# Second attention and expert blocks of a four-layer kernel: which semaphore GpSimd's sums wait for, where additions to x and routing work stand in VectorE's order, and which banks the first searches use

## Reference

```python
x = x + L0_xattn(ln(x), ctx, mask)        # one head, keys and values are ctx
x = x + L0_ffn(ln(x), ...)                # 32 experts of 96, top 8 of the router's logits, softmax over the chosen
x = x + L1_xattn(ln(x), ctx, ...)         # a decayed sum over ctx, one row for each of the 4 batches
x = x + L1_ffn(ln(x), ...)                # 8 experts of 176, top 2 of sigmoid(logits) + bias, and a shared part of 352
x = x + L2_xattn(ln(x), ctx, ...)         # 16 query heads, 4 key heads of 128, 1601 + 256 keys, causal over the 256
x = x + L2_ffn(ln(x), ...)                # 4 experts of 1024, top 1
x = x + L3_xattn(ln(x), ctx, ...)
x = x + L3_ffn(ln(x), ...)
```

```python
q = rms_norm(q, q_norm_w); k = rms_norm(k, k_norm_w)
q = q * cos + rotate_half(q) * sin;  k = k * cos + rotate_half(k) * sin
out = softmax(q @ [k_ctx, k].T * scale + mask) @ [v_ctx, v];  return out @ wo
```

## Time and profile before

| | |
|---|---|
| Median of 3 runs | 2511.46 us |
| The profiled execution | 2511.3 us, span 2509.4 us, granted clock 0.983 |
| TensorE matmul busy | 2353.1 us (94%) |
| VectorE, ScalarE, GpSimd busy | 1762.4, 1733.4, 1377.6 us |
| Chain that ended last | PE 49%, DVE 24%, issue 12%, ACT 11%, POOL 2% |
| Costliest lines of the chain | DVE 1461 6%, DVE 1508 5%, PE 1619 5% |
| GpSimd's sums, line 1298 | 400 of 1559 ns |

### The profile page before, as it was taken

One profiled execution on the slowest core, in us unless ns is written; L12 is line 12 of the kernel. 1 busy time (PEld: TensorE's weight loads), 2 busy tenths in 40 slices (PEclk: granted clock), 3 DMA queues, 4 the chain that ended last, 5 costly groups with the idle time before them and its releaser, 6 DMA issues.

```text
span 2509.4 us, 53706 instructions
## 1 busy us (share of the span) xinstructions
PE 2353.1 (94%) x19062; PEld 1629.6 (65%) x19123; DVE 1762.4 (70%) x3346; ACT 1733.4 (69%) x3784; POOL 1377.6 (55%) x942
## 2 busy tenths in 40 slices
PE   7989999989999999999999999999899899999997
PEld 5677777756777777777777777777656444444434
DVE  5455767667888888888888888889621467566546
ACT  2234444447878887888878788788711488888897
POOL 1045545425666766667666676667610478778500
PEclk9989999999999999999999999999999999999999
DMA  5122322230001000010000100001310200000100
GB/s 196 56 89 82 88 83 86 70 127 18 1 17 49 18 18 2 18 49 18 18 2 18 49 18 18 2 17 41 160 47 11 72 18 19 24 16 24 53 4 18
DMA packets 42366, 108.73 MB, mean 43 GB/s; under 512 B 5060, under 2 KB 25928, under 8 KB 36936
## 3 DMA queue, kind: packets, MB, share of 16 engines
q1 hardware_dynamic: 40312, 102.28, 12.1%
q0 software_dynamic: 768, 2.10, 0.3%
q10 hardware_dynamic: 1008, 0.79, 0.1%
HBM read 99.78 MB, written 4.98 MB: 42 GB/s over the span
## 4 chain that ended last, share of the span: by engine, by line
PE 49%; DVE 24%; issue 12%; ACT 11%; POOL 2%; DVEq 1%; DMA 1%; another core or an unknown queue 0%; ACTq 0%; SPq 0%; POOLq 0%
DVE l_plo L1461 6%; DVE l_mx L1508 5%; PE psum L1619 5%; PE psum L2763 4%; PE psum L2730 3%; PE psum L2127 3%; ACT l_p L2566 3%; PE psum L2696 3%; PE psum L513 2%; PE psum L514 2%; PE psum L515 2%; PE psum L374 2%; PE psum L393 2%; ACT l_p L1341 1%; PE psum L2137 1%
## 5 line engine op out<-in xcount | busy, mean ns | idle before, releaser
L1298 POOL TENSOR_TENSOR xn<-xn,l_p 128x512 f32<-128x512 f32 (+1 forms) x400 | 623.6, 1559 | 132.4 <-ACT l_p L1341 113.5
L1461 DVE TENSOR_TENSOR l_plo<-l_p,l_phi 128x512 fp32r<-128x512 f32 (+1 forms) x464 | 457.8, 987 | 32.9 <-ACT l_phi L1340 15.7
L2566 ACT ACTIVATE l_p<-psum 128x1024 f32<-128x1024 f32 x416 | 397.7, 1036 | 54.8 <-PE psum L2730 50.1
L1340 ACT ACTIVATE l_phi<-psum 128x512 fp32r<-128x512 f32 (+1 forms) x464 | 280.7, 605 | 142.0 <-PE psum L1667 72.1
L1508 DVE TENSOR_REDUCE l_mx<-psum 128x1 f32<-128x512 f32 (+2 forms) x512 | 299.7, 615 | 10.5 <-PE psum L1714 9.9
L1352 ACT ACTIVATE psum<-l_m 128x512 f32<-128x512 f32 x461 | 286.8, 624 | 6.1
L2541 POOL TENSOR_TENSOR l_rs<-l_ms,half_power 128x32 f32<-128x32 f32 x45 | 244.4, 5432 | 68.7 <-DVE l_ms L2591 58.8
L1341 ACT ACTIVATE l_p<-psum 128x512 f32<-128x512 f32 (+1 forms) x464 | 281.3, 606 | 0.0
L2763 PE MATMUL psum<-l_p,l_vs 64*32 64x256 f32 x6656 | 251.3, 378 | 6.9 <-POOL l_vs L2537 3.0
L1648 PE MATMUL psum<-l_qThi,l_kThi 128*128 128x512 f32 (+1 forms) x464 | 233.8, 504 | 1.0 <-ACT psum L1352 1.0
L1619 PE MATMUL psum<-l_w,l_ctx 128*128 128x256 f32 (+1 forms) x832 | 218.9, 386 | 1.3 <-DVE l_vlo L1501 0.6
(11 more groups left out here) (410 smaller groups left out, 5112.5 us busy)
## 6 DMA issues: line engine op xcount, KB each, us to landing
w_stage<-in_L_w_dram SPq DMA_DIRECT2D x76, 384.0 KB, 3.1
l_w<-in_L_w_qkv_dram SPq DMA_DIRECT2D x16, 1024.0 KB, 4.8
l_ct<-in_ctx_tiles_dram SPq DMA_DIRECT2D x52, 128.0 KB, 2.1
c_T<-in_ctx_T_dram SPq DMA_DIRECT2D x4, 1601.0 KB, 7.9
l_ctx<-in_ctx_T_dram SPq DMA_DIRECT2D x4, 1601.0 KB, 6.8
c_N<-in_ctx_dram SPq DMA_DIRECT2D x4, 1536.0 KB
s_wg<-in_L_gate_dram SPq DMA_DIRECT2D x4, 1024.0 KB, 11.5
s_wu<-in_L_up_dram SPq DMA_DIRECT2D x4, 1024.0 KB, 13.6
```

Of the source, the lines that this page charges most:

```text
L1298: g_.tensor_tensor(l2_acc[k][0:r, :], first[0:r, :], l2_p[c % 3][0:r, :], ALU.add)\
L1340: act.activation(l2_phi[c % 3][0:r, :], src, ACT.Exp).then_inc(l2_e, 1)
L1461: v.tensor_tensor(l2_plo[c % 3][0:r, :], l2_p[c % 3][0:r, :], l2_phi[c % 3][0:r, :].bitcast(F32), ALU.subtract)\
L2566: act.activation(l3_p[ring(odd, c)][:, :], psum[:, (c % 2) * 2 * BANK:(c % 2 + 1) * 2 * BANK], ACT.Exp, scale=float(D3) ** -0.5).then_inc( ...
```

## The change

GpSimd's sum of a step waits for VectorE's low part of that step, not for ScalarE's exponential. The additions of the late row (k = 1) stand ahead of `prepare` in VectorE's step. `route_weights` is cut in two, `route_weights` and `route_parts`, with a table entry "parts"; for block 2 the second stands one step later, for block 3 the first moves from step 13 to 12 and the second stands at 13. In blocks 0 and 3 TensorE turns the weights before `gate_up` of the second step, not behind it. The last twelve searches ahead of turn 0 use banks 3 to 6.

```diff
-                "acted": 12, "spread": 14, "weights": 16, "table": 17},
+                "acted": 12, "spread": 14, "parts": 14, "weights": 16, "table": 17},
...
-                "logits": 18, "route": 19, "acted": 19, "spread": 20, "weights": 22, "table": 23},
+                "logits": 18, "route": 19, "acted": 19, "spread": 20, "parts": 21, "weights": 22, "table": 23},
...
-                "logits": 11, "route": 11, "acted": 12, "spread": 13, "table": 13},
+                "logits": 11, "route": 11, "acted": 12, "spread": 12, "parts": 13, "table": 13},
...
         def route_weights(v, k):
...
             if name == "L0":
                 dve_steps.then(v, v.tensor_tensor(route, a, b, ALU.subtract))
-                dve_steps.then(v, v.tensor_reduce(r_sum[:, :], route, AX.X, ALU.add))
-                dve_steps.then(v, v.reciprocal(r_sum[:, :], r_sum[:, :]))
-                dve_steps.then(v, v.tensor_tensor(route, route, wide(r_sum[:, :], E), ALU.mult))
             else:
...
                 route_topk(v, E, 2, log)
+
+        def route_parts(v, k):
...
+            if name == "L0":
+                dve_steps.then(v, v.tensor_reduce(r_sum[:, :], route, AX.X, ALU.add))
+            else:
                 dve_steps.then(v, v.tensor_tensor(route, a, b, ALU.mult))
                 dve_steps.then(v, v.tensor_reduce(r_sum[:, :], route, AX.X, ALU.add))
                 dve_steps.then(v, v.tensor_scalar(r_sum[:, :], r_sum[:, :], 1e-12, None, ALU.max))
-                dve_steps.then(v, v.reciprocal(r_sum[:, :], r_sum[:, :]))
-                dve_steps.then(v, v.tensor_tensor(route, route, wide(r_sum[:, :], E), ALU.mult))
                 dve_steps.then(v, v.memset(r_route[:, :, E:E + 1], 1.0))
+            dve_steps.then(v, v.reciprocal(r_sum[:, :], r_sum[:, :]))
+            dve_steps.then(v, v.tensor_tensor(route, route, wide(r_sum[:, :], E), ALU.mult))
...
             if at_step("spread", new, i):
                 route_weights(v, new)
+            if at_step("parts", new, i):
+                route_parts(v, new)
...
-                    if not (late and i == 1):
-                        gate_up(k, m)
+                    gate_up(k, m)
                     if late and i == 0:
                         if m - 2 >= first:
                             down(m - 2)
-                        gate_up(k, m + 1)
                         turn_weights(pe, k)
...
-        FIVE_BANKS = [FIVE[at % 5] for at in range(LAST_ON_FIVE)] + TWO_BANKS[LAST_ON_FIVE:]
+        FOUR = (3, 4, 5, 6)
+        FIVE_BANKS = [FIVE[at % 5] for at in range(LAST_ON_FIVE)] + [FOUR[(at - LAST_ON_FIVE) % 4] for at in range(LAST_ON_FIVE, len(SHARED))]
+        FIRST_LAST_IN_3 = max(SHARED[at][1] for at in range(LAST_ON_FIVE, len(SHARED)) if FIVE_BANKS[at] == 3) + 1
...
-                g_.wait_ge(l2_e, g * (3 * NS) + (3 * c + 2))
+                g_.wait_ge(l2_lo, g * NS + (c + 1))
...
+                    for half in range(2):
+                        if g is not None and c == Y_AT[1][half] and not (isinstance(g, int) and g < 1):
+                            add_out(g - 1, 1, half)
                     if n is not None:
                         prepare(c, 1 - slot, n)
...
-                                if c == Y_AT[k][half]:
-                                    add_out(g - turns_ago, k, half, LAST_Y[k][half] if last_turn(g - turns_ago) else 7)
+                                if k == 0 and c == Y_AT[0][half]:
+                                    add_out(g, 0, half, LAST_Y[0][half] if last_turn(g) else 7)
...
-            if at < 0 and banks(n)[own] == 3:
+            if at < 0 and own >= LAST_ON_FIVE and isinstance(n, int) and n == 0:
+                pe.wait_ge(h_cp, HALF_CP[1])
+            elif at < 0 and banks(n)[own] == 3:
                 pe.wait_ge(l2_o, (n - 1) * TB + 1)
...
-                if c == 0 and g > 0:
-                    pe.wait_ge(l2_far, g * NM + LAST_IN_3)
+                if c == 0:
+                    pe.wait_ge(l2_far, (g * NM + LAST_IN_3) if not isinstance(g, int) or g > 0 else FIRST_LAST_IN_3)
```

More of the change, by code:

```diff
@@ L781, in route_weights @@
             name = BLOCKS[k][0]
-            E, n_slots = MOE[name][0], MOE[name][0] + (MOE[name][2] > 0)
+            E = MOE[name][0]
             a, b, log, route = (r[:, :, 0:E] for r in (r_a, r_b, r_log, r_route))
@@ L794, in route_weights @@
                 route_topk(v, E, 2, log)
+        def route_parts(v, k):
+            name = BLOCKS[k][0]
+            E, n_slots = MOE[name][0], MOE[name][0] + (MOE[name][2] > 0)
+            a, b, route = (r[:, :, 0:E] for r in (r_a, r_b, r_route))
+            if name == "L0":
+                dve_steps.then(v, v.tensor_reduce(r_sum[:, :], route, AX.X, ALU.add))
+            else:
                 dve_steps.then(v, v.tensor_tensor(route, a, b, ALU.mult))
@@ L900, in moe_vector @@
             route_weights(v, run[0])
+            route_parts(v, run[0])
             route_table(v, run[0])
```

## The result

| | before | after |
|---|---|---|
| median of the runs (5 each), us | 2511.86 | 2523.58 |
| lowest to highest, us | 2510.0 to 2513.19 | 2519.45 to 2526.77 |
| ratio to before, 95% interval | | 1.0046 [1.0031, 1.0061] |
| profiled execution, us; its span | 2511.3; 2509.4 | 2522.44; 2520.4 |

What follows compares the result with a forecast made beforehand. TensorE was taken as nearly full, so only its waits in expert blocks, before the attention and in steps 3 to 8 could be won. 2.5 + 2.5 + 3.2 + 1.3 + 5.6 = 15.1 off 2511.3: 2496.2 us; range 2483 to 2506.

Steps and rivals of the forecast that it cites:

- The step that failed: Attention: ScalarE's exponentials wait for sums three steps on but run five us ahead of TensorE, so delays are covered.
- the sum that now stands ahead of the power in step 17: Attention, step 17: the sum between low part and power delays l2_kn, so the transposes wait 0.3 us.
- Block 0: First expert block: earlier turning of the weights lets the third gate_up start earlier; 2.5 us won, range 0 to 2.5.
- Block 1: Expert block 1, step 20: cutting routing starts VectorE's multiplications 2.0 us earlier and the next gate_up 2.5 us earlier.
- the case that I had priced at 1.9: Block 1: the half clock comes all the same, down costs 1.35 more, turning's wait covers 0.7; 1.9 us won.
- Block 2 to 3: End of block 2: routing's first half in step 12 and turning ahead of gate_up win 3.2 us; 0 at half clock.
- Searches: Last twelve searches before turn 0: four banks let pieces run ahead of scores; 1.3 us won, ends 0 and 2.3.
- The additions: Attention, steps 3 to 8: line 1703 comes 0.9 us (even) or 1.6 to 2.0 (odd) earlier; step 8's low part waits instead.
- rival A: Attention: the wait only moves from line 1703 to step 8's low part; total gain 10.2, 2501 us; chance 0.24.
- Additions and sums together: Attention, steps 3 to 8: VectorE's chain to step 8's low part shortens, 0.7 us a turn, before step 17's cost.
- Rival D: Slower: GpSimd late at step 17's sum, power and product, transposes wait 2.1 us a turn; 2533 us; chance 0.04.
- My signs to look for: Expected: earlier expert blocks, line 1703's wait gone; wrong if over 1 us remains or exponentials wait for GpSimd and TensorE behind.

Runs made afterwards that it cites:

- the first experiment: The kernel after with all of GpSimd's sums waiting for the exponential again, additions still moved ahead: 2508.05 us, 0.998 of before.
- the sums alone: The kernel before with only GpSimd's sums made to wait for VectorE's low parts: 2539.88 us, 1.0103 of before.
- only sum 10 late: The kernel before with only the sum of step 10 waiting for VectorE's low part: 2529.05 us, 1.0067 of before.
- routing alone: The kernel before with only routing cut into two steps, the second gate_up left ahead of the turning: 2511.14 us, 0.9993 of before.
- moebanks: The kernel after with both attention parts (late sums, moved additions) undone, two-step routing and four banks kept: 2500.26 us, 0.9952 of before.
- the expert blocks alone: The kernel before with only two-step routing and the second gate_up behind the turning, search banks unchanged: 2506.43 us, 0.997 of before.
- the sums undone: The kernel after with GpSimd's sums waiting for the exponential again, all else as changed: 2508.05 us, 0.998 of before.
- the additions alone: The kernel before with only the late row's additions ahead of the preparing work: 2520.43 us, 1.0028 of before.
- best1: The kernel moebanks with only the sums of steps 20 to 24 waiting for VectorE's low parts: 2485.62 us, 0.9894 of before.
- best2: The kernel best1 with the sums of steps 7 and 8 waiting for low parts as well: 2492.09 us, 0.9917 of before.

## Why the prediction was wrong

**The step that failed** is this one: "ScalarE's exponentials wait for the sums three steps on and are five us ahead of TensorE, so their delays are covered." The first half is true. In the kernel after the exponentials are still 4.8 to 9.1 us ahead of their own third value products (means over the even turns, by step). But TensorE does not wait for the exponential. It waits for `l_vlo`, that for the copy `l_vhi`, and the copy stands behind the exponential in ScalarE's queue with no such lead: in turn 4 of the kernel before the `l_vlo` behind the exponential of step 14 ends 1.09 us before its `project`, and the one of the step before 0.05 us (922.10 and 922.15). Sum 11 pushed that exponential back by 2.0 us. I took the lead of an instruction for the slack of its engine. So the attention, which I had down as 5.6 us won, lost 21.7.

The second half of the same mistake is on GpSimd. I costed the sum that now stands ahead of the power in step 17, where TensorE waits for `l_kn`, and there I was right: 0.3 forecast, 0.24 measured. I did not cost the same insertion of sum 10 ahead of the power of step 9, because its `l_kn` has time. The sum of step 11 behind it has not: 2 us a turn, 30 in all, of which the late sums give half back elsewhere (15.5 net, by the first experiment).

Point by point:
- **Block 0**: 2.5 forecast, 2.7 measured (12.0 to 9.3), and 1.0 in the next step. In two other kernels with the old blocks (the sums alone, only sum 10 late) the first figure is 10.7 and the next step longer by as much; over three steps the gain is 3.4 to 3.7. Right in its mechanism, and a little low.
- **Block 1**: 2.5 taken, 1.6 measured. The half clock stayed on `down`, the case that I had priced at 1.9, and one product of routing took 1.15 us.
- **Block 2 to 3**: 3.2 taken, 3.0 and 1.05 behind it, and the same 4 us in every kernel with the new blocks. Right; both stretches ran at full clock. By the experiment with routing alone this comes from the order of `gate_up` and turning and hardly from the earlier multiplications.
- **Searches**: 1.3 forecast, 3.2 measured in moebanks, 2.3 of it against the expert blocks alone, which keep two banks. VectorE's gaps closed as argued. But the clock went with them, as the two fences below the list show, and all six kernels with two banks have some of this half clock; how much of the gain is the banks' and how much the clock's, no run separates.
- **The additions**: 19.5 us of waits gone, as forecast, and all given back to low parts, `l_qTlo` and `l_vlo`. That was rival A's mechanism ("the wait only moves from line 1703 to the low part of step 8"), which allowed a gain of 0.35 a turn. Measured without the late sums it is a loss: 0.71 (even) and 0.35 (odd) from moebanks to the sums undone, 0.83 and 1.12 from before to the additions alone, since the low parts of steps 10 to 12 are bound by VectorE too, and the first addition makes it idle.
- **Additions and sums together**: 0.7 a turn of gain was forecast for steps 3 to 8. From before to after these steps take 0.05 us more in even turns and 0.49 less in odd ones, so 0.2, below even rival A's 0.35. The real gain of the sums is in steps 21 and 24, 1.0 a turn, of which 0.35 are given back in steps 25 and 28, and with the additions ahead 0.8 in steps 9 to 12. I looked at neither; TensorE's waits there are small and many.
- **Rival D** (slower, GpSimd late) named the right engine and the right cause, an inserted sum ahead of a power. It had the wrong place, the power of step 17 instead of that of step 9, and the wrong waiter, and so a chance of 0.04. The time it gave, 2533, is 9 us above what came.

Busy time in 14 us of the searches, of the kernel before and then of the same work after (PE, PEld, DVE, ACT, POOL; granted clock; DMA):

```profile
557.00:571.00 14.00, 12.00 (x31) 7.70 (x32) 9.61 (x18) 2.68 (x5) 0.00 (x0) 0.52 0.00 1
```

```profile
549.00:563.00 14.00, 10.15 (x45) 6.88 (x46) 13.48 (x25) 4.70 (x9) 1.93 (x2) 1.00 0.03 12
```

TensorE worked there at half clock, 12.0 us for 31 matmuls, and VectorE waited for it; after, the clock is whole, 45 matmuls take 10.2 us and VectorE is full. In moebanks, with four banks too, the same window has a granted share of 0.88.

My signs to look for had the right question as their last words ("or if exponentials wait for GpSimd and TensorE behind them"): that is what the profile shows.

## What to carry to other kernels

When a wait is added, follow every instruction behind it on its engine to those who wait for *them*, and ask of each not how early its own result is but how early the next thing in that queue is. A wait that removes a collision belongs only where the delayed engine has nothing urgent next: the same edit cost 11 to 16 us on the sum of step 10 alone and won 14.6 in steps 20 to 24. And where an engine is without a gap over several steps, moving one of its operations forward moved TensorE's wait here, and did not remove it.

## What the runs showed that I had not expected

**A wait costs more than its length when the clock falls behind it.** In the kernels that keep the wait at line 1703, it is 2.0 us in each odd turn, and the clock falls to half behind it in some and not in others, with the same work on the same engines. Busy time in moebanks, turn 3 (two stretches from 816 us) and turn 5 (two from 974):

```profile
816.00:820.00 4.00, 1.96 (x9) 1.42 (x7) 3.84 (x8) 1.21 (x3) 3.71 (x4) 0.92 0.01 2
820.00:824.00 4.00, 4.00 (x13) 3.17 (x13) 4.00 (x5) 2.42 (x7) 3.14 (x2) 0.65 0.00 0
974.00:978.00 4.00, 1.96 (x9) 1.37 (x8) 3.84 (x8) 1.31 (x3) 3.63 (x4) 1.00 0.01 2
978.00:982.00 4.00, 3.48 (x17) 2.56 (x15) 4.00 (x4) 3.92 (x14) 3.84 (x3) 1.00 0.00 0
```

Step 6 to 7 takes 6.18 us in the one and 4.79 in the other. Of the six odd turns from 3 to 13 none was long in before, one in moebanks, two with only sum 10 late, three in best1, in experts_alone and with routing alone, four in best2, and none in the six kernels in which the second addition stands ahead, the kernel after among them, where the wait is gone. So the moved additions do win something, a cover against the half clock, worth 0.8 to 1.7 us in such a turn; where the wait is 2.94 (sums alone), step 6 to 7 was over 6.6 us in every one of them.
